# Three block steps per slot instead of two where attention ends, the first table three slots earlier, and two returns per dispatch

## Chip, cores and metric

One core of one Trainium2 chip runs the whole kernel. The metric is device time in microseconds (us) of one execution; lower is better. The kernel before takes 308.99 us, the median of 3 runs (307.54 to 309.55). A difference of about 1% (3 us) is the least that a measurement of this kernel tells from no change.

## What is computed

One transformer layer on x of shape 8 x 512 x 128, float32: causal linear attention without a softmax (16 heads of 8), then a mixture of 8 experts of which each token takes its best 2.

```python
def attn(x):                       # x is the layer norm of the input
    Q, K, V = proj(wq), proj(wk), proj(wv)                 # 16 heads of 8
    scores = einsum('bhld,bhsd->bhls', Q, K) * causal
    out = einsum('bhls,bhsd->bhld', scores, V)
    return out @ wo.T + wo_b

def ffn(x):                        # x is the layer norm of x + attn
    topk_p, topk_i = top_k(softmax(x @ Wg), 2)
    for e in range(8):
        ye = relu(xs @ W1[e] + b1[e]) @ W2[e] + b2[e]      # xs: rows sorted by expert
        y = y + (e_sorted == e) * ye
    return scatter_add(y * p)

x = x + attn(layernorm(x)); x = x + ffn(layernorm(x))
```

## The kernel before

**Tiles and slots.** The 4096 tokens are N = 32 tiles of 128, four to a batch, eight batches. Each engine has its own program, written by hand, and engines wait for one another by semaphores alone. The attention part of each program is a loop over slots s. A list of stages, each with a lag, says that in slot s the engine does stage f for tile s - lag (`tile_stages`); the stages stand in the order of the list. An engine does what its program says next, and waits there if it isn't ready. The slot numbers of two engines don't mean the same time: VectorE's slot s runs beside TensorE's and ScalarE's slot s + 3 or so.

**What a tile goes through.** VectorE multiplies outer products (`outer_product`, L614), TensorE sums them along the tokens (`running_sums`, L870, at lag 3), VectorE multiplies by q (`attend`, L623) and adds up (`attend_sum`, L636). TensorE transposes and projects (`o_transposed` L879, `project_out` L892, lag 7) and VectorE adds the residual (`add_residual`, L605, VectorE's lag 5). ScalarE then makes the second layer norm of the tile, from L446 to `rows_out` (L507), all at lag 10. TensorE transposes the rows (`transpose2`, L899, lag 10 as well) and computes the gate (L907, lag 11). Once per batch, VectorE does the softmax and the choice of two experts (`softmax_start`, `softmax_end`, `places`), TensorE the rank within each expert (`rank`, L919, lag 12), and ScalarE writes the weights into the rows (`chosen`, L473, lag 13).

**Dispatch.** GpSimd writes every tile's rows to the DRAM table `dispatched`, sorted by expert, with two indirect DMAs per tile (`dispatch`, L374). A dispatch waits for `chosen` of its batch. When all is written, each expert's region is whole; the table has 71 blocks of 128 rows. The first 32 of them (FIRST) hold only rows of the first five batches (EARLY = 5): the counts after batch 4 (`count`, L934, and `count_first`, L739) give a first table of block addresses (`first_table`, L744 to L750), so these blocks can be worked on while attention ends. `rest_table` does the same for the other 39 blocks, after the last batch.

**Blocks.** A block n goes through `load_block` (SyncE, L313, into one of G = 16 buffers `xt`), `transpose_x` (TensorE, L949), `xT_out` (ScalarE, L538), `hidden` (TensorE, L956), `hT_out` (ScalarE, L546), `output` (TensorE, L967 and L968), `y_weighted` (VectorE, L793) and `send_back` (GpSimd, L402: an indirect DMA to the DRAM table `returned`). VectorE copies the expert's first weight (`w1_out`, L788). Again each engine does these at lags, one `block_step(k)` after another: on TensorE hidden of block k-2, transpose_x of k, output of k-4; on ScalarE xT_out of k-1, hT_out of k-3. Steps -3 to -1 only read eight block addresses into registers (`registers`, `bias_registers`), as does every eighth step later. In TensorE's and ScalarE's slots from 36 on (`s >= N + 4`), and VectorE's from 33 on, STEPS = 2 block steps stand behind the tile stages of each slot; after the last slot the rest follow without tile stages.

```python
for s in range(-2, N + 13):                       # ScalarE, L555
    for lag, stage in tile_stages: ...
    if s >= N + 4:
        for _ in range(STEPS):
            block_step(block_stages, k)
            k += 1
```

**GpSimd's order** (L408 to L419) is one queue: in its slot s it dispatches tile s - 16, and from slot 39 on it sends blocks back behind the dispatch: two in slot 39 (behind tile 23), one in each later slot, and all that remain after the last dispatch (tile 31).

**SyncE's order** is one queue too: the loads of blocks 0 to 31, each with a wait for the return of block n - 16 which frees the buffer; then eight writes of padding behind the experts' regions (L302); then the loads of blocks 32 to 70, which wait for these writes and for all dispatches. At the end it waits for all returns, reads `returned` back (L321), VectorE adds (L824, L826), and ScalarE stores.

Of the kernel before, what the change touches and what calls it, by code (L numbers as in the profile page):

```python
# [36 lines left out]
def preln_linear_attention_moe(nc, x, w_qkv, b_qkv, w_o, b_o, w_gate, w1, b1, w2, b2, out):  # L37
    B, L, D = x.shape
    E, _, H = w1.shape
    T = L // P  # L40
    N = B * T
# [14 lines left out]
    EARLY = 5  # L56
    FIRST = (K * EARLY * L - E * (P - 1)) // P
    FIRST -= FIRST % READ
    REST = BLOCKS - FIRST
    STEPS = 2  # L60
    RING = 4
# [5 lines left out]
    with ExitStack() as ctx:  # L67
# [140 lines left out]
        att_mm, x2_done = sem("att_mm"), sem("x2_done")  # L208
# [117 lines left out]
        def _(pool):  # L326
# [81 lines left out]
            for s in range(N + 16):  # L408
                if s >= 16:
                    dispatch(s - 16)  # L410
                if s < N:
                    outer_product(s)
                    b2_split(s)
                more = 2 if s == T * (EARLY + 1) + 15 else 1 if s >= T * (EARLY + 1) + 16 else 0
                for _ in range(more):
                    send_back(sent)
                    sent += 1
# [4 lines left out]
        def _(act):  # L422
# [130 lines left out]
            deviation1(0)  # L553
            k = -3
            for s in range(-2, N + 13):  # L555
                for lag, stage in tile_stages:
                    if 0 <= s - lag < N:
                        stage(s - lag)
                if s >= N + 4:
                    for _ in range(STEPS):  # L560
                        block_step(block_stages, k)
                        k += 1
# [8 lines left out]
        def _(dve):  # L571
# [218 lines left out]
            def y_weighted(n):  # L790
# [6 lines left out]
                           (9, places), (2, state_out), (-2, outer_product)]  # L797
            k = -3
            for s in range(-2, N + 9):
                for lag, stage in tile_stages:  # L800
                    if 0 <= s - lag < N:
                        stage(s - lag)
                    if s == N and stage is add_residual:
                        count_first()
                if s == N:
                    first_table()
                elif s == N + 3:
                    left_by_first()
                if s > N:
                    for _ in range(STEPS):  # L810
                        block_step(block_stages, k)
                        k += 1
            for _ in range(2 * STEPS):
                block_step(block_stages, k)
                k += 1
# [13 lines left out]
        def _(pe):  # L829
# [55 lines left out]
            def project_out(g):  # L885
                wait(pe, oT_done, g + 1)
                wait(pe, x2_done, g)
                if g == N - T:
                    pe.wait_ge(cnt_read, 1)
                if g == 0:  # L890
                    pe.wait_ge(w_o_in, 16)
                pe.matmul(ps_att, oT[:, g % RING, :], wo_sb[:, :], start=True, stop=False)  # L892
                pe.matmul(ps_att, ones[:, :], bias_parts[:, 3 * D:4 * D], start=False, stop=True).then_inc(att_mm, 1)
# [66 lines left out]
            def output(n):  # L960
# [5 lines left out]
                for c in range(HC):  # L966
# [5 lines left out]
                           (-2, transpose1), (10, transpose2), (7, project_out), (12, rank)]  # L972
            k = -3
            for s in range(-2, N + 12):
                if s == N + 3:
                    pe.wait_ge(x2_done, N - T)
                    count(EARLY)
                for lag, stage in tile_stages:
                    if 0 <= s - lag < N:
                        stage(s - lag)  # L980
                if s >= N + 4:
                    for _ in range(STEPS):
                        block_step(block_stages, k)
                        k += 1
            for _ in range(STEPS):
                block_step(block_stages, k)
                k += 1
# [35 lines left out]
```

## Time and profile before

| | |
|---|---|
| median of 3 runs (lowest, highest) | 308.99 us (307.54, 309.55) |
| the profiled execution | 308.35 us |
| its span, first to last instruction | 306.6 us |
| mean granted TensorE clock | 0.916 of 2.4 GHz |
| busy share: TensorE, VectorE, ScalarE, GpSimd | 80%, 64%, 57%, 58% |
| attention alone | to about 150 us of the span |
| attention's last slots and the first 32 blocks | about 150 to 215 us |
| the other 39 blocks | about 220 to 284 us |
| reading back, adding, storing | to the end |

Times of rows count from the span's start. A row of a timeline gives start, duration, engine, line, operation, and in brackets how long the engine was idle before it and who released it. The profiled execution took 1.75 us more than its span, and is 0.64 us below the median of the runs.

### The profile page before, as it was taken

How to read it: one execution, taken by the hardware profiler on the slowest of the kernel's cores; microseconds unless marked ns; L12 is line 12 of the kernel's file. 1: busy time of each engine (PE TensorE's matmuls, PEld its weight loads, DVE VectorE, ACT ScalarE, POOL GpSimd, SP SyncE). 2: the span in 40 equal slices, each digit the busy share in tenths (PEclk: the TensorE clock that was granted, in tenths of full speed). 3: DMA queues.
4: the chain of work that ended last, by engine and by line, in shares of the span. 5: the costliest groups of instructions: out<-in, count | busy, mean ns of one | idle time of the engine just before them, and what ended most of it. 6: DMA issues, size and time to landing. Idle time of an engine off the chain costs nothing.

```text
span 306.6 us, 6357 instructions
## 1 busy us (share of the span) xinstructions
PE 244.9 (80%) x1392; PEld 176.5 (58%) x1392; DVE 195.5 (64%) x584; ACT 174.1 (57%) x701; POOL 179.1 (58%) x175
## 2 busy tenths in 40 slices
PE   0589999999999999987779976969399999896000
PEld 0234566666666666655557865857388778774000
DVE  5938999889998989999652456323143343342184
ACT  3243358888888888777678743445155556552000
POOL 3255492205868686876361777777777676676100
PEclk9999999999999999999566998899689999999655
DMA  7940000000111110111160222234443333211499
GB/s 208 310 145 0 1 2 0 0 4 17 37 37 35 38 36 28 43 36 55 34 169 17 62 74 66 70 84 127 132 116 103 92 89 87 68 47 36 155 356 310
DMA packets 32400, 25.50 MB, mean 83 GB/s; under 512 B 4305, under 2 KB 30169, under 8 KB 32364
## 3 DMA queue, kind: packets, MB, share of 16 engines
q1 hardware_dynamic: 23808, 14.52, 17.6%
q0 software_dynamic: 4320, 8.47, 8.4%
q10 hardware_dynamic: 4236, 2.10, 2.3%
q8 instruction: 14, 0.23, 0.3%
q14 instruction: 22, 0.18, 0.2%
HBM read 13.92 MB, written 11.61 MB: 83 GB/s over the span
## 4 chain that ended last, share of the span: by engine, by line
PE 53%; issue 13%; DVE 10%; DMA 9%; POOL 5%; ACT 4%; SPq 3%; ACTq 1%; POOLq 0%; DVEq 0%
PE ps L870 17%; PE ps L840 8%; PE ps L967 6%; PE ps L956 6%; POOL returned L402 4%; DMA back<-returned 3%; PE ps L879 2%; DMA returned<-y_sb,xt 2%; PE ps L892 2%; PE ps L842 2%; SPq L321 2%; DVE back L623 2%; POOL dispatched L374 2%; DVE o_sb L636 2%; PE ps L861 2%
## 5 line engine op out<-in xcount | busy, mean ns | idle before, releaser
L402 POOL DMA_INDIRECT returned<-y_sb,xt x71 | 70.4, 991 | 34.2 <-issue 20.9
L374 POOL DMA_INDIRECT dispatched<-rows,slot x64 | 64.3, 1005 | 37.8 <-ACT rows L473 21.5
L793 DVE TENSOR_SCALAR y_sb<-ps,xt 128x128 f32<-128x128 f32 x71 | 24.9, 350 | 73.4 <-PE ps L968 72.4
L870 PE MATMUL ps<-back,causal 128*128 128x512 f32 x128 | 62.8, 614 | 0.4 <-DVE back L614 0.4
L967 PE MATMUL ps<-w_sb,hT 128*128 x284 | 52.1, 309 | 6.4 <-DVE y_sb L793 4.8
L956 PE MATMUL ps<-xT,w_of 128*128 128x128 f32 x284 | 50.0, 302 | 2.7 <-ACT hT L546 1.9
L538 ACT ACTIVATE xT<-ps 128x128 f32<-128x128 f32 x71 | 19.6, 276 | 55.6 <-PE ps L949 54.4
L967 PEld LDWEIGHTS ps<-w_sb,hT 128*128 128x128 f32 x284 | 40.1, 204 | 19.0 <-issue 18.8
L358 POOL TENSOR_TENSOR back<-qkv 128x1024 f32<-128x1024 f32 x16 | 31.3, 1955 | 31.4 <-ACT qkv L494 31.1
L546 ACT ACTIVATE hT<-ps,b_col 128x128 f32<-128x128 f32 x142 | 43.9, 364 | 1.7 <-PE ps L956 1.4
L956 PEld LDWEIGHTS ps<-xT,w_of 128*128 128x128 f32 x284 | 40.0, 204 | 5.0 <-issue 4.1
L623 DVE TENSOR_TENSOR back<-ps,qkv 128x1024 f32<-128x1024 f32 x32 | 38.9, 1216 | 6.2 <-PE ps L870 6.2
L636 DVE TENSOR_REDUCE o_sb<-back 128x128 f32<-128x1024 f32 x32 | 38.7, 1208 | 0.0
L840 PE MATMUL ps<-wqkv_sb,xnT 128*128 128x384 f32 x64 | 29.3, 543 | 5.7 <-ACT xnT L485 5.7
L870 PEld LDWEIGHTS ps<-back,causal 128*128 128x128 f32 x128 | 22.3, 194 | 16.9 <-issue 15.8
L949 PE MATMUL ps<-ident,xt 128*128 128x128 f32 x71 | 20.8, 292 | 7.1 <-DMA xt<-dispatched 7.0
L494 ACT ACTIVATE qkv<-ps 128x384 f32<-128x384 f32 x32 | 15.5, 483 | 15.5 <-PE ps L842 15.5
L614 DVE TENSOR_TENSOR back<-qkv 128x1024 f32<-128x1024 f32 x16 | 21.2, 1327 | 0.0
L788 DVE COPY w_of<-w_sb 128x256 f32 x71 | 21.0, 298 | 0.1
L520 ACT ACTIVATE oT<-ps 128x128 f32<-128x128 f32 x32 | 8.9, 277 | 21.5 <-PE ps L882 16.5
L907 PEld LDWEIGHTS ps<-wg_sb,xn2T 128*128 128x128 f32 x64 | 12.3, 205 | 14.5 <-issue 10.2
L507 ACT ACTIVATE rows<-x_sb,norm 128x256 f32<-128x256 f32 x32 | 19.3, 603 | 0.4
(142 smaller groups left out, 415.9 us busy)
## 6 DMA issues: line engine op xcount, KB each, us to landing
xt<-dispatched SPq DMA_DIRECT2D x71, 65.0 KB, 2.0
back<-returned SPq DMA_DIRECT2D x8, 512.0 KB, 7.6
x_sb<-x SPq DMA_DIRECT2D x8, 256.0 KB, 5.0
out<-x_sb ACTq DMA_DIRECT2D x8, 256.0 KB, 6.6
returned<-y_sb,xt POOLq DMA_INDIRECT x71, 2.3
w_sb<-w SPq DMA_DIRECT2D x1, 1024.0 KB, 5.9
w_sb<-w SPq DMA_DIRECT2D x2, 512.0 KB, 7.2
dispatched<-rows,slot POOLq DMA_INDIRECT x64, 2.4
```

Source lines behind the costliest of these rows:

```text
L358: pool.tensor_tensor(outer[:, g % OUTER_RING, :].rearrange("p (h b a) -> p h b a", h=HEADS, b=DH), k, v, ALU.mult).then_inc(outer_pool, 1)
L374: pool.indirect_dma_start(out=dispatched[:, :], out_offset=bass.IndirectOffsetOnAxis(ap=slot[:, g * K + k:g * K + k + 1], axis=0), in_=row ...
L402: pool.indirect_dma_start(out=returned[:, :], out_offset=bass.IndirectOffsetOnAxis(ap=xt[:, n % G, D:D + 1].bitcast(I32), axis=0), in_=y_s ...
L546: act.activation(hT[:, n % W, c, :], ps_h[n % 2][:, c * P:(c + 1) * P], ACT.Relu, bias=b1_col[:, bass.ds(bias_at[n] + c, 1)]).then_inc(hT_ ...
L614: dve.tensor_tensor(outer[:, g % OUTER_RING, :].rearrange("p (h b a) -> p h b a", h=HEADS, b=DH), k, v, ALU.mult).then_inc(outer_dve, 1)
L623: dve.tensor_tensor(prod[:, g % 2, :].rearrange("p (h b a) -> p h b a", h=HEADS, b=DH), run, q, ALU.mult).then_inc(prod_done, 1)
L636: dve.tensor_reduce(o_sb[:, g % RING, :], prod[:, g % 2, :].rearrange("p (f a) -> p f a", a=DH), AX_X, ALU.add).then_inc(o_done, 1)
L793: dve.tensor_scalar(y_sb[:, n % G, :], ps_y, xt[:, n % G, D + 1:D + 2], None, ALU.mult).then_inc(y_done, 1)
L840: pe.matmul(ps_qkv, xnT[:, g % RING, :], wqkv_sb[:, :], start=True, stop=False)
L870: mm = pe.matmul(ps_run[g % 2][:, u, :], causal[:, :], outer[:, g % OUTER_RING, 512 * u:512 * (u + 1)], start=True, stop=True)
L956: mm = pe.matmul(ps_h[n % 2][:, c * P:(c + 1) * P], w1_of[:, n % W, c * P:(c + 1) * P], xT[:, n % W, :], start=True, stop=True)
L967: pe.matmul(ps_y, hT[:, n % W, c, :], w2_sb[:, c, bass.ds(w2_from[n], D)], start=(c == 0), stop=False)
```

## The change

STEPS becomes 3, so three block steps stand behind the tile stages of each slot. The steps -3 to -1, which only read registers, move to the end of the slot before the first block step on each engine, so that this slot holds steps 0 to 2. The counts of the first five batches and the first table are made three slots earlier on VectorE (count in slot 29, table in slot 30) and on TensorE (count in slot 32, ahead of all its tile stages, waiting for the residual of tile 24). GpSimd sends two blocks back behind each dispatch in its slots 39 to 43, then one in each of slots 44 to 47. After the last slot the number of steps ahead of the second count and table stays 2 on TensorE and 4 on VectorE.

```diff
--- before.py
+++ after.py
@@ -57,7 +57,9 @@
     FIRST = (K * EARLY * L - E * (P - 1)) // P
     FIRST -= FIRST % READ
     REST = BLOCKS - FIRST
-    STEPS = 2
+    STEPS = 3
+    FIRST_COUNT = N
+    BLOCKS_FROM = N + 4
     RING = 4
     OUTER_RING = 4
     QKV_RING = 3 * T
@@ -411,7 +413,8 @@
                 if s < N:
                     outer_product(s)
                     b2_split(s)
-                more = 2 if s == T * (EARLY + 1) + 15 else 1 if s >= T * (EARLY + 1) + 16 else 0
+                batch_after = T * (EARLY + 1) + 15
+                more = 2 if batch_after <= s <= batch_after + T else 1 if s > batch_after else 0
                 for _ in range(more):
                     send_back(sent)
                     sent += 1
@@ -551,12 +554,15 @@
                            (-1, xnT_out), (10, shift2_out), (6, qT_out), (10, rows_out), (-2, normalize), (7, oT_out), (13, chosen),
                            (-2, deviations_ahead)]
             deviation1(0)
-            k = -3
+            k = 0
             for s in range(-2, N + 13):
                 for lag, stage in tile_stages:
                     if 0 <= s - lag < N:
                         stage(s - lag)
-                if s >= N + 4:
+                if s == BLOCKS_FROM - 1:
+                    for before in (-3, -2, -1):
+                        block_step(block_stages, before)
+                if s >= BLOCKS_FROM:
                     for _ in range(STEPS):
                         block_step(block_stages, k)
                         k += 1
@@ -795,22 +801,25 @@
             block_stages = [(5, y_weighted), (0, w1_out), (-3, registers)]
             tile_stages = [(5, add_residual), (9, softmax_end), (1, attend_sum), (8, softmax_start), (0, attend), (0, scales_ahead),
                            (9, places), (2, state_out), (-2, outer_product)]
-            k = -3
+            k = 0
             for s in range(-2, N + 9):
                 for lag, stage in tile_stages:
                     if 0 <= s - lag < N:
                         stage(s - lag)
-                    if s == N and stage is add_residual:
+                    if s == FIRST_COUNT - 3 and stage is add_residual:
                         count_first()
-                if s == N:
+                if s == FIRST_COUNT - 2:
                     first_table()
                 elif s == N + 3:
                     left_by_first()
-                if s > N:
+                if s == BLOCKS_FROM - 4:
+                    for before in (-3, -2, -1):
+                        block_step(block_stages, before)
+                if s > BLOCKS_FROM - 4:
                     for _ in range(STEPS):
                         block_step(block_stages, k)
                         k += 1
-            for _ in range(2 * STEPS):
+            for _ in range(4):
                 block_step(block_stages, k)
                 k += 1
             rest_table()
@@ -885,7 +894,7 @@
             def project_out(g):
                 wait(pe, oT_done, g + 1)
                 wait(pe, x2_done, g)
-                if g == N - T:
+                if g == FIRST_COUNT - 7:
                     pe.wait_ge(cnt_read, 1)
                 if g == 0:
                     pe.wait_ge(w_o_in, 16)
@@ -970,19 +979,22 @@
             block_stages = [(2, hidden), (0, transpose_x), (4, output), (-3, registers)]
             tile_stages = [(3, running_sums), (11, gate), (5, q_transposed), (7, o_transposed), (5, sum_state), (-1, project),
                            (-2, transpose1), (10, transpose2), (7, project_out), (12, rank)]
-            k = -3
+            k = 0
             for s in range(-2, N + 12):
-                if s == N + 3:
-                    pe.wait_ge(x2_done, N - T)
+                if s == FIRST_COUNT:
+                    pe.wait_ge(x2_done, FIRST_COUNT - 7)
                     count(EARLY)
                 for lag, stage in tile_stages:
                     if 0 <= s - lag < N:
                         stage(s - lag)
-                if s >= N + 4:
+                if s == BLOCKS_FROM - 1:
+                    for before in (-3, -2, -1):
+                        block_step(block_stages, before)
+                if s >= BLOCKS_FROM:
                     for _ in range(STEPS):
                         block_step(block_stages, k)
                         k += 1
-            for _ in range(STEPS):
+            for _ in range(2):
                 block_step(block_stages, k)
                 k += 1
             count(B)

```

**GpSimd, from the first returns on.** The pairs of L374 are the two DMAs of a tile's dispatch, L402 a return; the first row is returns 0 and 1 behind tile 23, then come tiles 24 and 25. Before:

```order
L402 DMA returned<-y_sb,xt 8192x128 [waits y_done] x2
L374 DMA dispatched<-rows,slot 33920x130 [waits chosen_done,slot_done,rows_done]
L374 DMA dispatched<-rows,slot 33920x130
L402 DMA returned<-y_sb,xt 8192x128 [waits y_done]
L374 DMA dispatched<-rows,slot 33920x130 [waits chosen_done,slot_done,rows_done]
L374 DMA dispatched<-rows,slot 33920x130
L402 DMA returned<-y_sb,xt 8192x128 [waits y_done]
```

After (the lines are two further down in the file):

```order
L404 DMA returned<-y_sb,xt 8192x128 [waits y_done] x2
L376 DMA dispatched<-rows,slot 33920x130 [waits chosen_done,slot_done,rows_done]
L376 DMA dispatched<-rows,slot 33920x130
L404 DMA returned<-y_sb,xt 8192x128 [waits y_done] x2
L376 DMA dispatched<-rows,slot 33920x130 [waits chosen_done,slot_done,rows_done]
L376 DMA dispatched<-rows,slot 33920x130
L404 DMA returned<-y_sb,xt 8192x128 [waits y_done] x2
```

Each dispatch of tiles 24 to 27 now has two returns behind it, and these returns stand behind that dispatch as before. Tiles 28 to 31 have one each, and the 58 others follow.

**ScalarE, one slot's block steps.** From the rows of tile 29 (`rows_out`) to the next slot. Before, two steps, each an `xT_out` and one block's `hT_out` in two halves:

```order
L507 ACTIVATE rows<-x_sb,norm2 128x2x128 [waits x2_done,norm2_done]
L538 ACTIVATE xT<-ps 128x128 [waits TX_done]
L546 ISA [waits w_ffn,h_mm]
L546 ACTIVATE hT<-ps,b1_col 128x128
L546 ISA
L546 ACTIVATE hT<-ps,b1_col 128x128
L538 ACTIVATE xT<-ps 128x128 [waits TX_done]
L546 ISA [waits h_mm]
L546 ACTIVATE hT<-ps,b1_col 128x128
L546 ISA
L546 ACTIVATE hT<-ps,b1_col 128x128
L446 ACTIVATE unread,mean2<-x_sb 128x128 [waits x2_done]
```

After (three lines further down), from the same rows of tile 29 to the third step's `xT_out`; its two `hT_out` and then the next slot follow:

```order
L510 ACTIVATE rows<-x_sb,norm2 128x2x128 [waits x2_done,norm2_done]
L541 ACTIVATE xT<-ps 128x128 [waits h_mm,TX_done]
L549 ISA [waits y_mm,h_mm]
L549 ACTIVATE hT<-ps,b1_col 128x128
L549 ISA
L549 ACTIVATE hT<-ps,b1_col 128x128
L541 ACTIVATE xT<-ps 128x128 [waits h_mm,TX_done]
L549 ISA [waits y_mm,h_mm]
L549 ACTIVATE hT<-ps,b1_col 128x128
L549 ISA
L549 ACTIVATE hT<-ps,b1_col 128x128
L541 ACTIVATE xT<-ps 128x128 [waits h_mm,TX_done]
```

In TensorE's program each of these steps is a hidden, a transpose_x and an output. Between `chosen` of tiles 20 to 23 and `chosen` of tiles 24 to 27, ScalarE did xT_out of blocks 0 to 3 and hT_out of 0 and 1 before; now it does xT_out of blocks 0 to 10 and hT_out of 0 to 8.

**TensorE, the count of the first five batches.** The rank of batch 4 (its last row is L926), then the running sums of tile 29 (L870). Before:

```order
L924 MATMUL ps<-picked,ones 128x32
L926 MATMUL ps<-region_h,ones 128x32
L870 MATMUL ps<-back,causal 128x512 [waits prod_done,outer_dve]
L870 MATMUL ps<-back,causal 128x512
L907 MATMUL ps<-wg_sb,xn2T 128x8 [waits shift_done,qkv_done,xn2T_done]
```

After (nine lines further down), with the count at L943:

```order
L933 MATMUL ps<-picked,ones 128x32
L935 MATMUL ps<-region_h,ones 128x32
L943 MATMUL ps<-picked,ones 1x8 [waits placeof_done,before_done,x2_done]
L879 MATMUL ps<-back,causal 128x512 [waits prod_done,outer_dve]
L879 MATMUL ps<-back,causal 128x512
L916 MATMUL ps<-wg_sb,xn2T 128x8 [waits shift_done,qkv_done,xn2T_done]
```

The count, which waits for `x2_done` (the residual of tile 24), now stands ahead of the running sums of tile 29. Before, it stood three slots later, where no running sums follow.

## Rows read from the trace of the kernel before

**Rows 1.** Chain that ended last: start, duration (us), what.

```profile
207.97 2.26 DMA returned<-y_sb,xt
...
215.13 2.73 DMA dispatched<-padding
...
219.95 0.47 PE ps L949
...
283.59 2.10 DMA returned<-y_sb,xt
```

**Rows 2.** Timeline of GpSimd: start, us, engine, line, operation [idle before <-releaser].

```profile
149.65 0.96 POOL L374 DMA_INDIRECT dispatched<-rows,slot  x1 [4.86 <-ACT rows L473]
...
165.49 0.99 POOL L402 DMA_INDIRECT returned<-y_sb,xt  x1 [6.05 <-DVE y_sb L793]
...
169.27 0.99 POOL L402 DMA_INDIRECT returned<-y_sb,xt  x1 [2.79 <-DVE y_sb L793]
170.57 0.96 POOL L374 DMA_INDIRECT dispatched<-rows,slot  x1 [0.31 <-DVE y_sb L793]
...
200.21 1.00 POOL L402 DMA_INDIRECT returned<-y_sb,xt  x1 [0.30 <-issue]
...
207.97 0.98 POOL L402 DMA_INDIRECT returned<-y_sb,xt  x1 [0.30 <-DVE y_sb L793]
```

**Rows 3.** Timeline of ScalarE, starts of its slots 37, 40, 41.

```profile
148.46 0.84 ACT L473 ACTIVATE rows<-top,grec 128x2 f32<-128x2 f32 x4
149.91 0.31 ACT L446 ACTIVATE unread<-x_sb 128x128 f32<-128x128 f32 x1 [0.61 <-issue]
...
162.93 0.32 ACT L446 ACTIVATE unread<-x_sb 128x128 f32<-128x128 f32 x1
...
165.31 0.84 ACT L473 ACTIVATE rows<-top,grec 128x2 f32<-128x2 f32 x4
...
167.21 0.62 ACT L546 ACTIVATE hT<-ps,b_col 128x128 f32<-128x128 f32 x2
167.71 0.32 ACT L446 ACTIVATE unread<-x_sb 128x128 f32<-128x128 f32 x1
```

**Rows 4.** Timeline of TensorE.

```profile
130.90 1.96 PE L870 MATMUL ps<-back,causal 128*128 128x512 f32 x4
...
145.27 0.19 PE L919 MATMUL ps<-picked,earlier 128*128 128x32 bf16 x1
...
148.66 0.45 PE L899 MATMUL ps<-ident,rows 128*128 128x128 f32 x1
150.63 0.77 PE L892 MATMUL ps<-wo_sb,oT 128*128 128x128 f32 x2 [1.52 <-DVE x_sb L605]
...
157.91 0.42 PE L949 MATMUL ps<-ident,xt 128*128 128x128 f32 x1
...
165.46 0.48 PE L899 MATMUL ps<-ident,rows 128*128 128x128 f32 x1 [0.46 <-ACT rows L507]
...
221.26 1.17 PE L956 MATMUL ps<-xT,w_of 128*128 128x128 f32 x4
...
223.39 1.07 PE L956 MATMUL ps<-xT,w_of 128*128 128x128 f32 x4
...
224.91 0.67 PE L956 MATMUL ps<-xT,w_of 128*128 128x128 f32 x4
...
226.30 0.67 PE L956 MATMUL ps<-xT,w_of 128*128 128x128 f32 x4
```

**Rows 5.** Timeline of VectorE.

```profile
133.69 0.28 DVE L605 TENSOR_TENSOR x_sb<-ps,x_sb 128x128 f32<-128x128 f32 x1
...
147.10 0.15 DVE L744 TENSOR_SCALAR cnt_i<-cnt_i 1x8 int32<-1x8 int32 x1
...
150.21 0.27 DVE L605 TENSOR_TENSOR x_sb<-ps,x_sb 128x128 f32<-128x128 f32 x1
```

**Rows 6.** Busy time by stretch: us, PE, PEld, DVE, ACT, POOL busy (x count), granted clock, DMA share, GB/s.

```profile
150.00:160.00 10.00, 7.75 (x30) 6.05 (x30) 4.34 (x32) 6.85 (x31) 7.30 (x8) 0.53 0.56 136
```

## The prediction

> **What bounds the kernel now.** I read the chain that ended last first, from the end, then the timelines of the engines that it passes, and last the busy time by stretch. The end of the chain is rigid. Return 15 starts at 207.97 and lands 2.26 us later; SyncE may then load block 31, writes the eight paddings, whose last starts at 215.13 and lands 2.73 us later, loads block 32, and TensorE transposes it at 219.95. The last return starts at 283.59 and lands 2.10 us later; reading back, adding and storing come behind [rows 1]. From 219.95 on TensorE does a block every 1.39 us (226.30 - 224.91) once its clock is up [rows 4]: 39 blocks are 54.2 us, and the pipeline's fill and a few stalls make up the 63.6 us to 283.59. GpSimd could do the 55 returns behind return 15 in 55 x 1.29 = 71 us, until 278.9: 4.7 us of slack. So whatever moves return 15 moves the end by as much.
>
> What sets return 15 is GpSimd. It works without a hole from 170.57, the first dispatch of tile 24, to return 15 at 207.97: 29 DMAs (16 of dispatches, 13 returns) in 37.4 us, 1.29 us each, where waits between them are 0.30 us or so [rows 2]. Ahead of that it has holes: 6.05 us before return 0 and 2.79 us before return 1 [rows 2]. The dispatch of tile 24 stood behind return 1; its own condition, the weights of its batch (`chosen`), was begun at 165.31 on ScalarE, 5 us earlier [rows 3]. The question of this change is thus when the dispatch of tile 24 starts. Behind it the same 29 DMAs follow (13 returns again, only elsewhere among the dispatches), so return 15 comes 37.4 us later as before.
>
> **Part 1, count and table sooner.** The table takes 150.21 - 147.10 = 3.1 us on VectorE [rows 5]. Moved ahead of the last two attention tiles it costs these what it cost the residual of tile 28 before: nothing net for that residual, but 3.1 us for all between, the choice of experts of tiles 20 to 23 among it. The count now stands ahead of TensorE's running sums of tile 29. Those started at 130.90 [rows 4]; the count waits for the residual of tile 24, done at 133.69 + 0.28 = 133.97 [rows 5]. The sums, 1.96 us, then end at about 136.0, and VectorE, which wanted them about 1.1 us after 133.89, loses 1.0 us. Queued behind the waiting count are also the gate and the projection of that slot, which VectorE needs later still. I take 1.0 us; the bounds are 0.3 us (VectorE had spare work I overlooked) and 2 us (the sums of tile 30 are late too).
>
> What the earlier table gives: nothing by itself. Its first loads can start some 6 us sooner, but the first block is transposed only in TensorE's slot 36, and returns wait behind the dispatches of tiles 20 to 23.
>
> **Part 2, to the start of slot 37.** TensorE's rank of tiles 20 to 23, at 145.27, stands behind the table now: 145.3 + 3.1 + 1.0 = 149.4. From the rank to the end of the transpose of tile 26's rows are 148.66 + 0.45 - 145.27 = 3.8 us [rows 4], and the register read that now lies between costs 0.6 us, as the hole of 0.61 us on ScalarE shows for the same read [rows 3]: the projection of tile 29 starts at 153.8, where it started at 150.63. It takes 0.77 us; then blocks 0 and 1 are transposed, 0.42 us each, each with an eviction of some 0.3 us by ScalarE (half of a pair's 0.62) [rows 3, 4]. ScalarE's slot 37 starts behind the second of these evictions, at 154.6 + 1.5 = 156.1. Before, it waited for no block there and started at 149.91 [rows 3].
>
> **Part 3, the slots with three steps.** ScalarE and TensorE turn in a ring. ScalarE's slot begins with the second norm (L446 to the rows); TensorE transposes these rows (165.46) and only then does the slot's block steps; ScalarE's last step needs TensorE's last but one; its `hT_out` ends at 167.8, and the next slot begins at 167.71 [rows 3, 4]. The slot from 162.93 took 4.8 us, 0.8 of it `chosen`: 4.0 us without. With two steps one of TensorE's steps lies in this ring, with three there are two. A step is 1.39 us at full clock and 223.39 - 221.26 = 2.13 us at half [rows 4]. TensorE's granted clock was 0.53 of 2.4 GHz in 150 to 160, so mostly its lower level of 1.2 GHz, with the engine busy for 7.75 of 10 us [rows 6]; I take half clock for slot 37 and full clock for 38 and 39. The three slots are 3 x 4.0 + 2.1 + 1.4 + 1.4 = 16.9 us, and the projections of tiles 30 and 31, now also ahead of the steps in the ring, add 0.8 and 0.4 us: 18.1 us. Slot 40 starts at 174.2. `chosen` of tiles 24 to 27 comes 2.4 us later (165.31 - 162.93), at 176.6, and the dispatch 1.2 us behind it (149.65 - 148.46) [rows 2, 3]: tile 24 at 177.8, not 170.57, **7.2 us later**.
>
> The bounds: at full clock throughout, some 2.3 us less, 4.9 us later; at half clock throughout, 1.5 us more, 8.7 us later. A second count agrees: `chosen` stands behind the hidden layers of blocks 0 to 8 and no longer only 0 and 1, seven blocks more at 1.39 us or above, which is 9.7 us behind 165.31, and gives 176.2 for tile 24.
>
> A page of the Trainium skill bears on the clock (TensorE: Matmul & The Clock Gate, "The HAM clock gate"): the gate is set "based on how busy the PE has been recently". The third step fills TensorE, so by that rule the clock would come back sooner than in rows 6, and the sum would be nearer its full-clock end. No row here shows a slot with three steps.
>
> **Part 4, two returns per dispatch.** Returns 2 and 3 now stand behind tile 24's dispatch, 4 and 5 behind tile 25's. They can't go before it. Blocks 2 and 3 will have been weighted long before 177.8, and GpSimd idles: the dispatches of tiles 20 to 23 start near 149.65 + 4.1 = 153.8, their eight DMAs and returns 0 and 1 last until 166.5, and then there is a hole of 11 us. Afterwards returns 4 to 9 come earlier relative to tile 24, which feeds blocks 18 to 25 in time, but return 15 is behind the same work. No gain.
>
> **Part 5, the second table.** The count stands behind step 25, not 14. Block 25 needs return 9, 15 DMAs or 19.3 us behind tile 24's start, then 2.3 us of landing and 2.1 us of load (from 217.86 to 219.95, rows 1). With some 5 us for count and table this is done 29 us behind tile 24's start; the first load that needs it comes 39.7 us behind. Its stall of VectorE is covered by the wait for returns. Cost nothing; without that cover, at most the table's own 4 us.
>
> **Sum.** 308.35 us is the profiled execution, 306.6 us its span and 1.75 us around it. + 7.2 = 315.6 us. That execution is 0.64 us below the median of the runs, so the median should be **316.2 us**.
>
> **The rivals.**
> *The ring doesn't take the third step* (chance 0.14): it lies beside ScalarE's norm work, and slots stay at 4.0 us. For it: TensorE was idle for 2.2 of 10 us [rows 6]. Against: ScalarE's program has the third step's eviction ahead of the next norm. Tile 24 would be at 156.1 + 12.0 + 1.2 + 2.4 + 1.2 = 172.9, 2.3 us late: 311.3 us, no difference that can be told.
> *GpSimd's holes close* (0.10): the earlier table brings block 0 forward and ScalarE reaches `chosen` in time. Tile 24 then follows return 1 at 166.5, 4.1 us sooner: 304.9 us. For it: 8.8 us of holes in rows 2. It decides as soon as `chosen` of tiles 24 to 27 begins before 169.4, that is 1.2 us ahead of 170.57. Against it are seven blocks more ahead of `chosen`.
> *A second hole* (0.14): the dispatch of tile 28 waits for `chosen` of the last batch, which stands behind block 22's eviction; block 22 needs return 6, 12.9 us behind tile 24's start, so 17.3 us until it is transposed and 19.2 us until tile 28 may go. GpSimd gets there after 16 DMAs, 20.6 us. The margin is 1.4 us; if the gate, softmax and rank of the last batch take 4 us more, 2.6 us are added to the 7.2: 318.8 us.
> *The forecast* has the remaining 0.62.
>
> **Chances.** About 1% is what a measurement here tells from no change. Slower by over 1%: the forecast and the second hole, 0.76. Within 1%: 0.14. Faster: 0.10. The range from 309.0 to 320.0 us takes in both bounds of the forecast, the first rival and the second hole; the faster case and what lies beyond are left out.
>
> **What would show it.** Right, if in the new profile GpSimd shows a hole of about 11 us, released by ScalarE's `chosen`, before the dispatch of tile 24 at 176 to 179; if return 15 follows 37 us behind and block 32 is transposed 49.4 us behind; if ScalarE's starts of L446 in slots 38 to 40 are 5.5 to 7 us apart; and if VectorE waits about 1 us for the sums of tile 29. Wrong, if that dispatch has no hole before it, if slots remain at 4 to 5 us, or if the distance from return 15 to the end changes from 100.4 us.

## Result and the profile after

The changed kernel takes 320.26 us, the median of 4 runs (317.65 to 320.79), beside 308.65 us before; the ratio is 1.0367, 95% interval 1.0308 to 1.0425: slower by 3 to 4%. The forecast was 316.2 us in a range of 309.0 to 320.0: the direction and the mechanism are right, the time is just outside the range, and the size was too small. The profiled execution took 317.65 us (span 315.9 us) and is the fastest of all; the others lie close together at 320.2 to 320.8 us, and a part of what sets them apart is one of the findings below.

GpSimd's timeline after the change, its rows that answer to [rows 2] (start, us, operation, idle before and who ended it):

```profile
154.53 0.96 POOL L376 DMA_INDIRECT dispatched<-rows,slot  x1 [6.30 <-ACT rows L476]
...
164.68 0.99 POOL L404 DMA_INDIRECT returned<-y_sb,xt  x1 [0.35 <-issue]
168.51 0.99 POOL L404 DMA_INDIRECT returned<-y_sb,xt  x1 [2.84 <-DVE y_sb L799]
179.68 0.96 POOL L376 DMA_INDIRECT dispatched<-rows,slot  x1 [10.18 <-ACT rows L476]
...
200.20 0.96 POOL L376 DMA_INDIRECT dispatched<-rows,slot  x1 [0.30 <-issue]
...
216.88 0.98 POOL L404 DMA_INDIRECT returned<-y_sb,xt  x1 [0.30 <-issue]
```

The first row is the dispatch of tile 20, the next two are returns 0 and 1, 179.68 is tile 24, 200.20 tile 28 and 216.88 return 15. The hole before the dispatch of tile 24 is there, 10.18 us long (11 us were forecast), and L476, `chosen`, ended it. Tile 24 goes at 179.68, 9.1 us later than the 170.57 of [rows 2], and return 15 starts 37.2 us behind it (37.4 before).

ScalarE's timeline, the starts of its slots 37 to 40 (L449) between `chosen` of tiles 20 to 23 and `chosen` of tiles 24 to 27 (both L476), which answer to [rows 3]:

```profile
153.35 0.84 ACT L476 ACTIVATE rows<-top,grec 128x2 f32<-128x2 f32 x4
...
155.88 0.30 ACT L449 ACTIVATE unread<-x_sb 128x128 f32<-128x128 f32 x1
...
163.86 0.31 ACT L449 ACTIVATE unread<-x_sb 128x128 f32<-128x128 f32 x1
...
169.96 0.32 ACT L449 ACTIVATE unread<-x_sb 128x128 f32<-128x128 f32 x1
...
176.09 0.32 ACT L449 ACTIVATE unread<-x_sb 128x128 f32<-128x128 f32 x1
...
178.47 0.84 ACT L476 ACTIVATE rows<-top,grec 128x2 f32<-128x2 f32 x4
```

Slot 37 starts at 155.88 (forecast 156.1). The slots take 7.98, 6.10 and 6.13 us, 20.2 in sum, where 18.1 were forecast.

The chain that ended last, from return 15 on, answers to [rows 1]:

```profile
216.88 2.26 DMA returned<-y_sb,xt
...
224.04 2.47 DMA dispatched<-padding
226.66 1.81 DMA xt<-dispatched
228.52 0.47 PE ps L958
...
301.12 10.47 DMA back<-returned
```

Block 32 is transposed at 228.52, 8.6 us later than before, and the reading back is waited for from 301.12. From return 15 to the end of the span are 99.0 us, before 98.6 (306.6 - 207.97). (The forecast's 100.4 us were counted to the end of the execution; so counted it is 100.8.) So the loss arises before return 15, as the forecast had it: 8.9 of the 9.3 us of span.

TensorE's timeline, around the count (L943), and the projection of tile 29:

```profile
133.88 0.17 PE L943 MATMUL ps<-picked,ones 128*1 128x8 bf16 x1 [2.98 <-DVE x_sb L611]
133.98 1.98 PE L879 MATMUL ps<-back,causal 128*128 128x512 f32 x4
...
153.79 0.65 PE L901 MATMUL ps<-wo_sb,oT 128*128 128x128 f32 x2
```

TensorE waits 2.98 us at the count, and the running sums follow at 133.98. The projection of tile 29 starts at 153.79; 153.8 was forecast.

### The profile page after: what moved, and what is told of

Its sections match the earlier page's. It is cut to its first block, busy times and chain, and to the rows that moved or that the text cites. A ratio compares the mean times of both kernels' runs of the same rounds, so it can differ in the third digit from the quotient of the medians.

```text
span 315.9 us, 6358 instructions
## 1 busy us (share of the span) xinstructions
PE 249.4 (79%) x1392; PEld 181.1 (57%) x1392; DVE 196.2 (62%) x584; ACT 174.4 (55%) x701; POOL 179.3 (57%) x175
## 4 chain that ended last, share of the span: by engine, by line
PE 56%; issue 13%; DVE 8%; DMA 7%; ACT 6%; POOL 5%; SPq 3%; ACTq 1%; POOLq 0%; DVEq 0%
PE ps L879 17%; PE ps L849 7%; PE ps L976 7%; PE ps L965 7%; POOL returned L404 4%; DMA back<-returned 3%; PE ps L888 3%; PE ps L901 2%; PE ps L958 2%; SPq L323 2%; PE ps L851 2%; PE ps L870 2%; PE ps L891 2%; DMA returned<-y_sb,xt 1%; PE ps L908 1%
## 5 line engine op out<-in xcount | busy, mean ns | idle before, releaser
L976 PE MATMUL ps<-w_sb,hT 128*128 x284 | 53.7, 317 | 3.8 <-DVE y_sb L799 2.3
L965 PE MATMUL ps<-xT,w_of 128*128 128x128 f32 x284 | 53.0, 314 | 2.3 <-ACT hT L549 1.2
L976 PEld LDWEIGHTS ps<-w_sb,hT 128*128 128x128 f32 x284 | 41.9, 212 | 15.4 <-issue 15.0
L965 PEld LDWEIGHTS ps<-xT,w_of 128*128 128x128 f32 x284 | 42.6, 215 | 4.7 <-issue 3.5
L879 PEld LDWEIGHTS ps<-back,causal 128*128 128x128 f32 x128 | 22.3, 195 | 17.0 <-issue 15.9
L958 PE MATMUL ps<-ident,xt 128*128 128x128 f32 x71 | 22.1, 311 | 11.3 <-DMA xt<-dispatched 10.6
```

Source lines behind the costliest of these rows:

```text
L879: mm = pe.matmul(ps_run[g % 2][:, u, :], causal[:, :], outer[:, g % OUTER_RING, 512 * u:512 * (u + 1)], start=True, stop=True)
L958: pe.transpose(ps_x, xt[:, n % G, 0:D], ident[:, :]).then_inc(TX_done, 1)
L965: mm = pe.matmul(ps_h[n % 2][:, c * P:(c + 1) * P], w1_of[:, n % W, c * P:(c + 1) * P], xT[:, n % W, :], start=True, stop=True)
L976: pe.matmul(ps_y, hT[:, n % W, c, :], w2_sb[:, c, bass.ds(w2_from[n], D)], start=(c == 0), stop=False)
```

## Experiments

Four kernels took the change apart, one at a time. "Before" was 308.8 us beside these four.

**Three steps alone.**

```diff
-    STEPS = 2
+    STEPS = 3
...
-            for _ in range(2 * STEPS):
+            for _ in range(4):
...
-            for _ in range(STEPS):
+            for _ in range(2):
```

> The kernel before with three steps per slot alone: steps -3 to -1 in slot 36, so chosen of tiles 24 to 27 stands behind the hidden layers of blocks 0 to 5. Theory (what ScalarE's chosen waits for sets the dispatch of tile 24, and that sets the end): slots 38 and 39 take about 6 us each instead of 4.4 and 4.9, block 0 and 1 are evicted ahead of slot 38; tile 24 goes at about 173.5 instead of 170.57, so 311.5 us. Rival (the third step costs all of the loss by itself, wherever the table stands): 318 to 320 us. Rival (the third step is free, the early table costs everything): 308.7 us.

Measured: 314.35 us, ratio 1.0177 (1.0125 to 1.0228). Its GpSimd timeline, the dispatches of tiles 24 and 28:

```profile
173.38 0.96 POOL L374 DMA_INDIRECT dispatched<-rows,slot  x1 [4.04 <-ACT rows L473]
...
192.65 0.96 POOL L374 DMA_INDIRECT dispatched<-rows,slot  x1 [4.04 <-ACT rows L473]
```

Tile 24 goes at 173.38, as reckoned (173.5), 2.8 us late. But a second hole of 4.04 us stands before tile 28: with one return per dispatch GpSimd comes there after 12 DMAs, not 16, and ahead of `chosen`. That is the second hole of the forecast, in this kernel instead of the changed one. Without the usual 0.3 us the hole adds 3.7 us, and 2.8 + 3.7 is the 6.5 us by which return 15 is late (214.44); the time is 5.6 us more. I had not carried the rival over to this kernel when I expected 311.5.

**Early count and table alone.**

```diff
-                    if s == N and stage is add_residual:
+                    if s == N - 3 and stage is add_residual:
...
-                if s == N:
+                if s == N - 2:
                     first_table()
...
-                if g == N - T:
+                if g == N - 7:
                     pe.wait_ge(cnt_read, 1)
...
-                if s == N + 3:
-                    pe.wait_ge(x2_done, N - T)
+                if s == N:
+                    pe.wait_ge(x2_done, N - 7)
```

> The kernel before with the count and the first table three slots earlier, two steps per slot, registers in place, one return per dispatch. Theory: the choice of experts of tiles 20 to 23 is late by the table's 3.1 us and the count's 1.0 to 1.5 us, the dispatch of tile 20 by about 4.5 us, ScalarE's slots 37 to 40 by about as much, tile 24 goes at about 174.5: 312.5 us. Rival (the early table brings block 0 forward and costs nothing else): 308 us or less.

Measured: 315.25 us, ratio 1.0206 (1.0144 to 1.0268). The early table is no gain, it is a loss of 6.5 us by itself, more than the 4 expected. In its profile the dispatch of tile 20 is at 156.93 and that of tile 24 at 177.87, both 7.3 us late, and the granted clock in 130 to 140 is 0.83 where it was 1.00 before. Of the 7.3 us, 1.25 lie ahead of the residual of tile 24 (134.94), where the two programs are the same; 2.5 lie between the residuals of tiles 24 and 25, and 3.6 behind them, where the table was reckoned as 3.1. Tile 24 isn't held by `chosen` here, begun at 172.67, but goes directly behind return 1 (176.57), as in the kernel before.

**Two returns per dispatch alone.**

```diff
-                more = 2 if s == T * (EARLY + 1) + 15 else 1 if s >= T * (EARLY + 1) + 16 else 0
+                more = 2 if T * (EARLY + 1) + 15 <= s <= T * (EARLY + 1) + 15 + T else 1 if s > T * (EARLY + 1) + 15 else 0
```

> The kernel before with two returns behind each dispatch in GpSimd's slots 39 to 43. Theory: the same DMAs stand between the dispatch of tile 24 and return 15, so no change: 308.7 us, within 1 us, though TensorE's wait for block 25 (2.15 us) goes and the dispatch of tile 31 is 5 us later. Rival (returns 2 to 9 sooner let TensorE run on): 306.5 us. Rival (the later last dispatch delays block 32): 311 us or more.

Measured: 309.36 us, ratio 1.0018 (0.9985 to 1.0050): no change, as part 4 of the forecast had it.

**The changed kernel with two steps.**

```diff
-    STEPS = 3
+    STEPS = 2
```

> The changed kernel with two steps per slot; early table, early register reads and two returns stay. Theory: slots 37 to 39 lose one TensorE step each (2.1, 1.4, 1.4 us) and slot 36 one transpose and eviction (0.9 us): tile 24 goes at about 174 instead of 179.68, and the time falls by 5.7 us, to about 314.5 us. Rival (the early table and the reads are the whole loss): 319 to 320 us. Rival (the third step is the whole loss): 309 us.

Measured: 317.54 us, ratio to before 1.0281 (1.0229 to 1.0332), so 2.7 us less than the changed kernel, not 5.7. Its ScalarE slots show a part of why (starts of slots 37 to 40):

```profile
158.84 0.30 ACT L449 ACTIVATE unread<-x_sb 128x128 f32<-128x128 f32 x1
...
165.57 0.31 ACT L449 ACTIVATE unread<-x_sb 128x128 f32<-128x128 f32 x1
...
172.17 0.31 ACT L449 ACTIVATE unread<-x_sb 128x128 f32<-128x128 f32 x1
...
176.56 0.32 ACT L449 ACTIVATE unread<-x_sb 128x128 f32<-128x128 f32 x1
```

Slots 37 to 39 take 17.7 us in sum with two steps and 20.2 with three: 2.5 us less, where 4.9 were expected. Slot 38 alone takes 6.60 us with two steps and 6.10 with three. Busy time by stretch goes with that, first of this kernel and then of the changed one (columns as in [rows 6]), in each the stretch 160 to 170 and then slot 38:

```profile
160.00:170.00 10.00, 7.57 (x31) 6.45 (x31) 1.79 (x11) 5.70 (x24) 6.36 (x7) 0.50 0.34 93
...
165.57:172.17 6.60, 5.07 (x26) 4.38 (x25) 1.74 (x11) 4.10 (x18) 2.01 (x3) 0.56 0.09 30
```

```profile
160.00:170.00 10.00, 8.87 (x59) 7.72 (x59) 3.15 (x16) 6.69 (x28) 5.40 (x6) 0.86 0.14 43
...
163.86:169.96 6.10, 4.97 (x36) 3.98 (x35) 2.74 (x15) 4.75 (x20) 2.45 (x3) 1.00 0.11 34
```

With two steps TensorE's clock stays at its lower level of 1.2 GHz all through 160 to 170, with three it is mostly at 2.4 GHz. In a second profile of the changed kernel, shown below, slot 38 takes 6.22 us at a clock of 0.95. So in these profiles the third step pays a part of its price back. This is the rule of the Trainium skill that the forecast weighed (TensorE: Matmul & The Clock Gate, "The HAM clock gate"), and the trace agrees: 0.86 with TensorE busy for 8.87 us, 0.50 with it busy for 7.57 us. Over all profiles of kernels like these the agreement is looser: in 160 to 170 the clock is 0.50 to 0.66 with two steps and 0.65 to 0.88 with three. The rest of what is missing lies ahead of the slots: slot 37 starts at 158.84, 3.0 us later than in the changed kernel's profile, where it was expected 0.9 us sooner. Of this, 1.1 us lie ahead of the residual of tile 24 (134.61, not 133.54), where the programs are the same, and the rest behind the wait at the count, as the next kernel shows.

The next four kernels start from the changed one. The kernel before took 308.48 us beside them.

**The changed kernel again**, unchanged, for a second profile.

> The changed kernel unchanged, for a second profile. The first one was 317.65 us, the other four runs 320.2 to 320.8. Theory: in those, TensorE's wait of 3 us ahead of the running sums of tile 29 lets the granted clock fall, so that the sums run at 1.2 GHz: a profile of about 320.4 us shows a clock below 1.00 in 130 to 140 and more than 6 us from the residual of tile 24 to that of 25 (4.93 us in the first). Rival (the 2.7 us arise later, between slots 37 and 44 or in the second hole at tile 28): the same 4.9 us, and a hole before the dispatch of tile 28.

Measured: 320.93 us over two runs, ratio to before 1.0386 (1.0304 to 1.0468); the profiled one took 320.32 us. The residuals of tiles 24 and 25 and the product that waits for the running sums, on VectorE:

```profile
134.39 0.28 DVE L611 TENSOR_TENSOR x_sb<-ps,x_sb 128x128 f32<-128x128 f32 x1
...
137.28 1.23 DVE L629 TENSOR_TENSOR back<-ps,qkv 128x1024 f32<-128x1024 f32 x1 [1.05 <-PE ps L879]
...
140.44 0.28 DVE L611 TENSOR_TENSOR x_sb<-ps,x_sb 128x128 f32<-128x128 f32 x1
```

The same two residuals in the first profile of the changed kernel, and that of tile 25 in the kernel before (tile 24 is at 133.69 there [rows 5]):

```profile
133.54 0.28 DVE L611 TENSOR_TENSOR x_sb<-ps,x_sb 128x128 f32<-128x128 f32 x1
...
138.47 0.28 DVE L611 TENSOR_TENSOR x_sb<-ps,x_sb 128x128 f32<-128x128 f32 x1
```

```profile
137.48 0.28 DVE L605 TENSOR_TENSOR x_sb<-ps,x_sb 128x128 f32<-128x128 f32 x1
```

The busy time by stretch of the second profile, followed by that of the first:

```profile
130.00:140.00 10.00, 6.83 (x37) 4.97 (x36) 7.51 (x20) 3.87 (x18) 4.09 (x4) 0.83 0.06 20
```

```profile
130.00:140.00 10.00, 6.48 (x35) 4.17 (x36) 9.01 (x18) 5.46 (x25) 4.87 (x5) 1.00 0.06 18
```

From residual to residual it is 6.05 us, against 4.93 in the first profile and 3.79 before (137.48 - 133.69). TensorE waited the same 2.98 us at the count in both. In the first profile its clock stayed up, here it fell, and the sums of tile 29 (2.42 us, not 1.98) and the work behind them ran in part at the lower level, just when VectorE stood waiting. The execution is 2.7 us longer, but only 1.1 us of that are the clock between these residuals; 0.85 lies ahead of the residual of tile 24, where nothing was changed, and the rest in small parts behind them. No hole stands before tile 28. The first profile is the lucky one: of the six profiles with this wait of 2.98 us ahead of the sums (the changed kernel twice, the early table alone, the changed kernel with two steps, and below that with the hole filled and that with `chosen` earlier) it alone has a clock of 1.00 in 130 to 140. The five others have 0.69 to 0.83 and 6.05 to 7.41 us from residual to residual. All profiles without this wait have 1.00. So the common case pays for the clock too.

**The count ahead of the projection of tile 25.**

```diff
                 if g == FIRST_COUNT - 7:
+                    count(EARLY)
                     pe.wait_ge(cnt_read, 1)
...
-                if s == FIRST_COUNT:
-                    pe.wait_ge(x2_done, FIRST_COUNT - 7)
-                    count(EARLY)
```

> The changed kernel with TensorE's count of the first five batches directly ahead of the projection of tile 25 in the same slot, so that it no longer stands ahead of the running sums of tile 29. Theory: the wait of 3 us and the fall of the clock behind it go; 1 us and, in most runs, 2.7 us less: 316.5 us. Rival (the count's place costs 1 us as reckoned): 319.3 us.

Measured: 318.37 us, ratio to before 1.0297 (1.0229 to 1.0366), about 2 us less than the changed kernel. TensorE's wait of 2.98 us is gone from the trace and its clock in 130 to 140 is 1.00; residual to residual is 4.61 us (134.65 to 139.26). The time is between the two expectations: VectorE still waits for its own round trip over the count (0.65 us), and the clock falls in 140 to 150 instead (0.87 there, 0.95 in the first profile of the changed kernel).

**GpSimd's hole filled.**

```diff
-                more = 2 if batch_after <= s <= batch_after + T else 1 if s > batch_after else 0
+                more = 7 if s == batch_after else 2 if batch_after < s <= batch_after + T else 1 if s > batch_after else 0
```

> The changed kernel with seven returns behind tile 23, two behind each of tiles 24 to 27 and one behind each of 28 to 31: returns 2 to 6 fill GpSimd's hole of 10 us. Theory (return 15 sets the end): return 15 starts at about 203 instead of 216.9, then TensorE's own blocks and the dispatches are the bound, block 32 at about 217 instead of 228.5: 309 us. Rival (the slots with three steps cost TensorE the time, whatever GpSimd's order): 319 to 320 us.

Measured: 309.12 us, ratio to before 1.0023 (0.9984 to 1.0062). One number in GpSimd's program takes back the whole loss of 11 us. GpSimd's timeline, returns 2 to 6 in the former hole and then tile 24:

```profile
171.55 0.98 POOL L404 DMA_INDIRECT returned<-y_sb,xt  x1 [0.38 <-issue]
173.10 0.98 POOL L404 DMA_INDIRECT returned<-y_sb,xt  x1 [0.57 <-issue]
176.33 0.98 POOL L404 DMA_INDIRECT returned<-y_sb,xt  x1 [2.25 <-DVE y_sb L799]
177.72 0.98 POOL L404 DMA_INDIRECT returned<-y_sb,xt  x1 [0.41 <-issue]
179.11 0.98 POOL L404 DMA_INDIRECT returned<-y_sb,xt  x1 [0.41 <-issue]
181.38 0.96 POOL L376 DMA_INDIRECT dispatched<-rows,slot  x1 [1.29 <-ACT rows L476]
...
204.45 1.00 POOL L404 DMA_INDIRECT returned<-y_sb,xt  x1 [0.30 <-issue]
```

The last row is return 15, 12.4 us earlier than in the first profile of the changed kernel, though tile 24 is 1.7 us later. The chain that ended last shows the next bound, the last dispatch:

```profile
214.83 2.28 DMA dispatched<-rows,slot
217.31 1.86 DMA xt<-dispatched
219.21 0.33 PE ps L958
```

Block 32 is transposed at 219.21, not 228.52. The slots with three steps and the early table are all still there, so what they cost the changed kernel they cost it through what stands waiting in GpSimd's queue. They aren't free for all that: the last dispatch goes at 214.83, 15.9 us later than in the kernel before (198.95), and now sets block 32. Whether the kernel before would gain from a better order of returns too is a question of its own, and stays open below.

**`chosen` a slot earlier** for tiles 24 to 31.

```diff
+            def chosen_ahead(g):
+                if g >= T * (EARLY + 1):
+                    chosen(g)
...
-                           (-1, xnT_out), (10, shift2_out), (6, qT_out), (10, rows_out), (-2, normalize), (7, oT_out), (13, chosen),
+                           (-1, xnT_out), (10, shift2_out), (6, qT_out), (10, rows_out), (-2, normalize), (7, oT_out), (12, chosen_ahead), (13, lambda g: None if g >= T * (EARLY + 1) else chosen(g)),
```

> The changed kernel with ScalarE's chosen of tiles 24 to 27 and of 28 to 31 at the end of the tile stages of slots 39 and 43 instead of 40 and 44. Theory: the dispatch of tile 24 goes at about 173.7 instead of 179.7, that of tile 28 at about 195.5 instead of 200.2, and return 15 is 4.7 us earlier, bound by the second: 315.5 us. Rival (tile 24 alone decides): 6 us less, 314 us. Rival (GpSimd isn't the bound): 320 us.

Measured: 316.11 us, ratio to before 1.0239 (1.0175 to 1.0302), 4.2 us less than the changed kernel. GpSimd's dispatches of tiles 24 and 28:

```profile
176.08 0.96 POOL L376 DMA_INDIRECT dispatched<-rows,slot  x1 [4.87 <-DVE slot L701]
...
197.88 0.96 POOL L376 DMA_INDIRECT dispatched<-rows,slot  x1 [1.59 <-DVE slot L701]
```

A second hole of 1.59 us opens, and tile 28 bounds the rest, as expected. But both dispatches now wait for the rows' places in the table, which VectorE computes (`slot`), so tile 24 goes at 176.08 and not at 173.7, and tile 28 at 197.88 and not at 195.5.

**Toward a version that beats both.** Three kernels: the kernel before with one return behind tile 23 instead of two; the kernel before with `chosen` a slot earlier and fewer returns ahead of tile 24; and the changed kernel with all three repairs. The edits of GpSimd's line in the first two (the second also has the edit of the table of steps just shown; the third has that edit too, the count ahead of the projection of tile 25, and returns put into the hole):

```diff
+                more = 1 if s >= T * (EARLY + 1) + 15 else 0
```

```diff
+                more = 0 if s < T * (EARLY + 1) + 17 else 1 if s == T * (EARLY + 1) + 17 else 2 if s < T * (EARLY + 2) + 16 else 1
```

> The kernel before with one return behind tile 23 instead of two: the dispatch of tile 24 no longer stands behind return 1, whose block is weighted only at 168.05. Theory: tile 24 goes at 166.8 instead of 170.57, with one more return behind it, so return 15 is 2.5 us earlier and so is the end: 306.1 us. Rival (return 1 was no wait that counts): 308.5 us.

> The kernel before with chosen of tiles 24 to 27 and of 28 to 31 a slot earlier on ScalarE, and on GpSimd no return behind tiles 23 and 24, one behind 25, two behind 26 and 27, then one each. Theory: tile 24 goes at about 163 instead of 170.57 and return 15 starts at about 203 instead of 207.97; TensorE's blocks to 31 are then as late as the returns, so block 32 gains some 5 us: 303.5 us. Rival (TensorE or the second table is already the bound at block 32): 306 to 308.5 us.

> The changed kernel with all three repairs: the count ahead of the projection of tile 25, chosen a slot earlier for tiles 24 to 31, and seven returns behind tile 23, two behind 24 to 27. Theory: 309.1 us of the filled hole, less 1 to 2 us for the count and about 2 us for the last batch's dispatches, then bound by GpSimd's returns at the end: 306 us. Rival (all three remove the same wait): 309 us.

> b_chosen once more, beside the kernel before. In its first comparison the kernel before itself took 355.6 us, with TensorE and VectorE held up between blocks, so GpSimd had waits of its own in all of the block part and its order could matter little. Theory: where the kernel before takes about 308.6 us and GpSimd works without a hole from tile 24 to return 15, b_chosen has tile 24 at about 163, return 15 near 203, block 32 some 5 us earlier: 303.5 us. Rival (TensorE or the second table is the bound at block 32 by then): 306 to 308.5 us.

These ran on other chips (0 and 10) than the eight kernels above (8 and 1), beside a kernel before that itself took 355.61 us (29 runs), and 356.76 us at the second try (17 runs), not 308.6. Measured: 355.83 us, ratio 1.0022 (0.9989 to 1.0056) for the one return; 353.43 us, ratio 0.9953 (0.9919 to 0.9988), and at the second try 353.52 us, ratio 0.9942 (0.9911 to 0.9974), for `chosen` earlier; 355.07 us, ratio 0.9982 (0.9943 to 1.0022) for the three repairs, of whose ten executions one took 589.67 us, for a cause that isn't known. In the first of these kernels GpSimd's timeline looks different from [rows 2]: GpSimd waited 50.4 us for weighted blocks, 21 times, where it was 13.3 us, 13 times, in the kernel before. So the expectations, which were for a GpSimd that works without holes, aren't tested by these runs. What can be said is that the second kernel gains about half a per cent in both tries, below what I call a difference. Whether it gains 5 us beside a kernel of 308.6 us wasn't measured.

## Why the prediction was right, and where its size was off

**What bounds the kernel.** Right, and shown by filling GpSimd's hole: with slots and table left as changed, return 15 went from 216.88 to 204.45 and the time from 320 to 309 us. The forecast of the time was 4 us too low, and the two steps of its sum that were too small are the count (Part 1) and the slots in the ring (Part 3).

**Part 1, the count: 1.0 us, bounds 0.3 to 2.** In the first profile right: the product of tile 29 starts at 135.99 (before 135.02). In the common case mis-sized. The residuals of tiles 24 and 25 are 6.05 us apart in the second profile, 2.3 us more than before, and 7.4 us apart (134.61 to 142.02) in the profile of the changed kernel with two steps. I counted the wait and not what it does to the clock of the work behind it. The register reads that moved ahead of the residual of tile 28 cost about what was reckoned: VectorE was idle for 0.60 us there.

**Part 2, the start of slot 37.** Right in the first profile, in part by luck: rank at 149.83 (149.4), projection at 153.79 (153.8), slot 37 at 155.88 (156.1). The rank is 0.4 us late and the way from it to the projection 0.4 us short (3.96, reckoned as 3.8 + 0.6), for TensorE shows no hole of 0.6 us for the register read there. In the second profile slot 37 starts at 158.17.

**Part 3, three steps in the ring.** The mechanism is right, the slots were 18.1 us and are 20.2. Slot 37 has 1.1 us of the difference. TensorE's gate and `o_transposed` stand ahead of the transposed rows there and ran at half clock, so that this transpose came at 159.73, 1.4 us behind the end of the rows at 158.36; I had taken 4.0 us for the rest of the ring from slot 40 of the kernel before, which ran at half clock too (0.50 from 162.93 to 167.71) but has no `o_transposed`; there the transpose came 0.06 us behind the rows. Slot 39 has 0.7 us, where a rank and a late weighting of a block (0.36 us) stand. That is the other mis-sized term.

**Part 4, returns.** Right: nothing by themselves. But they had a worth that the forecast didn't name: they keep the second hole shut. With three steps and one return per dispatch it was 4.04 us long, with two it was nil. The margin was reckoned as 1.4 us; it was about 0.6 in the first profile (`chosen` of the last batch at 198.37, 1.2 us to the dispatch, tile 28 at 200.20).

**Part 5, the second table.** Right: its 4 us don't appear on the chain.

**Sum.** Tile 24 was forecast 7.2 us late, is 9.1 us late in the first profile and 11.7 in the second. The forecast for the profiled execution was 315.6 us, it took 317.65. Of the 2.7 us more in the second profile 1.1 are the clock behind the count and 0.85 were there before anything had changed. The rival of a ring that doesn't take the third step fell (slots of 6 to 8 us), and so did closing holes (10.18 us).

**One by one.** Steps +5.6 us, table +6.5 us, returns +0.6 us (not told from none); that is 12.7 in sum, and the whole change costs 11.6. That these lie near each other is partly luck, for the parts aren't independent: 3.7 us of the first are the second hole, which the changed kernel doesn't have, and the third step taken out of the changed kernel gives back 2.7 us, not 5.6. What each part costs depends on what else is there; that it all arises ahead of return 15 doesn't: in the profiles of the kernel before, of steps or table alone, of the changed kernel (twice) and of it with two steps, the span ends 98.4 to 99.0 us behind the start of return 15.

## What to carry to other kernels

When one engine's queue feeds a ring of buffers, look at what stands in its order behind an instruction that can be late: a wait there stops everything queued behind, whether ready or not, and here the larger remedy was to put the ready work ahead of it (one number, 11 us), not to hurry the producer (`chosen` a slot earlier, 4 us). More work per slot moves every once-per-batch step later by a slot's growth times the slots ahead of it; check who waits for that step. And price a new wait on TensorE twice, once as idle time and once as half clock for what follows.

## What I had not expected of the hardware

The same program with the same wait of 2.98 us ahead of the running sums kept the granted clock at 1.00 in one execution and dropped to 0.83 in 130 to 140 in another, with 1.1 us more between two residuals. Six of the seven recorded executions of the changed kernel lie at 320 us or above, and only the first profiled one at 317.65. Four more kernels with the same wait were profiled, and in all of them the clock fell (0.69 to 0.83). What decides it was not tried.

The last comparisons ran at 355.6 us for the kernel before, 15% more. There is no profile of the kernel before from these runs; in that of the kernel with one return behind tile 23, attention is as fast as ever up to the residual of tile 25 (139.02), the dispatch of tile 20 is already 6.3 us late (155.94), and return 0 is 11.4 us late (176.88). Over its span TensorE had holes put down to no wait that the profile shows (41.2 us ahead of weight loads of L967, 18.8 us in the kernel before), and VectorE waited 29.2 us for something that the profile doesn't name. What causes it was not tried and stays open.
